# A linear-attention block with its feed-forward on one core: biases folded into the weights, one Relu pass per engine, and the first half reordered

## The chip, the core and the metric

One core of a Trainium2 chip. Its engines run side by side, each with its own queue of instructions in program order: TensorE (PE; matmuls into the banks of PSUM, the accumulator memory, 2 KB per partition each), VectorE (DVE), ScalarE (ACT), GpSimd (POOL) and SyncE (SP), which here issues all DMAs. They meet at semaphores: an instruction adds to one when it ends, and `wait_ge` holds a queue until a count is reached. The metric is the device time of one execution in microseconds; lower is better.

## The reference

```python
xn = _layernorm(x, axis=-1)                                  # x: 8 batches, 1024 tokens, 256 channels, fp32
qkv = (xn @ qkv_w + qkv_b).reshape(b, n, 3, H, D)            # 16 heads of 16
q, k = _l2norm(q), _l2norm(k)
kv = jnp.einsum('bhnd,bhne->bhde', k, v)                     # no softmax
out = jnp.einsum('bhnd,bhde->bhne', q, kv) ... @ proj_w + proj_b
h = jax.nn.relu(xn @ W1 + b1)                                # 1024 wide
return x + out + (h @ W2 + b2)
```

## The kernel before

Work goes in halves `s` of a batch (16 halves, 512 tokens, four tiles of 128); the even half of batch `b` has `u` = 0, the odd one `u` = 1. Each engine has a function `body(b)` that holds one batch in hand-written order; batch 0 and the last are written out, those between run in a loop. In batch 0 the flag `opening` marks its first half.

Every product is made in three: a value is split into `_hi` (rounded to the fast 32-bit format, by a copy) and `_lo` (the rest, by a subtraction), and `product` (L798 on) sums hi·hi, hi·lo and lo·hi. So nearly every tile takes a copy on ScalarE and a subtraction on VectorE or GpSimd before TensorE can use it.

For a half: VectorE takes the variance of x (`variance`) and writes xn (`normalise`, L602, a subtraction and a multiplication per tile); ScalarE makes xn_hi, GpSimd xn_lo (L295). VectorE transposes 32x32 blocks (L609) and SP moves them into place with 16 DMAs (L254); ScalarE and VectorE split xT. The feed-forward goes in eight chunks `j` of 128: `ffn_up` writes W1's chunk times xT into one of two `w_bank`s, ScalarE applies Relu with the bias twice, into h_hi (L444) and back into the bank (L445), VectorE subtracts to h_lo (`h_low`), and `ffn_down` adds h times W2 into `o_bank`. `ffn_up(j)` waits for `h_low(j - 2)`, and `ffn_down(j)` for `h_low(j)`. `query_key(s + 1, ., t)` makes q and k of the next half, tile by tile, into `v_bank`, between the chunks; VectorE adds the bias (L641), ScalarE squares, VectorE sums (L645), `bound` (L651), a root, and `divide` (L663) for k and then for q. q's blocks take the same way by DMA (`transpose_q`, then qT_hi on ScalarE, qT_lo on GpSimd, L332); k is split (k_lo, GpSimd, L307) and summed over the tokens (GpSimd, L315 and L321).

v is never made. `gather` (after chunk 2) sums G = xnᵀk in `g_bank`. In the odd half `key_value` (after chunk 4) makes Wvᵀ G, with two products with `ones` for the sum of k over tokens; ScalarE scales that sum with v's bias (L462), `mask_kv` on VectorE (L675 on) adds it, masks heads and splits; `project` (after chunk 6) multiplies by proj_w, m is split, and `attend` closes the batch with q times m for both halves; VectorE adds the results to y_sb (L694, L705), to which GpSimd added the output's biases (L300), and SP stores them.

At the start (L927 on) TensorE multiplies the identity 17 times, transposes half 0, multiplies it 7 times again, and then makes q and k of half 0 before the first chunk of the feed-forward. SP loads x, wqk, its bias spread over 128 partitions, W1, x of half 1, b1 (element by element) and W2.

## Time and profile before

| | us |
|---|---|
| median of three runs | 637.21 (634.02 to 637.76) |
| the profiled execution | 637.44, its span 635.7 |
| TensorE busy | 583.1 (92%) |
| VectorE busy | 484.0 (76%) |
| ScalarE busy | 285.3 (45%) |
| GpSimd busy | 230.2 (36%) |
| DMA, mean | 71 GB/s |

"Busy" is the time in which an engine has an instruction in work; matmuls overlap, so their durations add up to more than that. Busy shares are of the whole span; the stages are what the groups of rows below are for.

### The profile page before, as it was taken

The numbers are of one execution on the slowest core, as the hardware profiler recorded it, in microseconds if no ns is written. First come the engines' busy times: TensorE is split into PE (matmuls) and PEld (weight loads), VectorE is DVE, ScalarE is ACT, GpSimd is POOL, SyncE is SP. The second block draws the span as 40 slices with busy tenths as digits, with TensorE's granted clock in tenths as the row PEclk, the third lists the DMA queues.
The fourth block names the chain that finished last, engine by engine and source line by source line (L and its number), as shares of the span: only waits on it lengthen the run. The fifth ranks groups of instructions, "written<-read, shape, count | busy, mean of one in ns | idle before, by whom it ended". The sixth has DMA issues, their size and how long they took to land.

```text
span 635.7 us, 10583 instructions
## 1 busy us (share of the span) xinstructions
PE 583.1 (92%) x3648; PEld 522.8 (82%) x3648; DVE 484.0 (76%) x869; ACT 285.3 (45%) x500; POOL 230.2 (36%) x153
## 2 busy tenths in 40 slices
PE   7269999999999998999899999899998999899996
PEld 7259788988888887898788988898877988789896
DVE  5976886968869697887878788696887969785633
ACT  4434526354443645445363543635354463553540
POOL 3633552334313453024533155134440345311360
PEclk9779999999999999999999999999999999999998
DMA  8315122250322503224131422125031241212111
GB/s 248 82 41 143 18 40 61 74 143 17 78 57 54 144 14 76 74 37 128 29 70 66 124 42 66 33 77 144 15 76 51 58 108 19 43 70 38 63 34 66
DMA packets 80355, 44.85 MB, mean 71 GB/s; under 512 B 71376, under 2 KB 73168, under 8 KB 80336
## 3 DMA queue, kind: packets, MB, share of 16 engines
q1 hardware_dynamic: 80336, 44.60, 27.7%
q8 instruction: 11, 0.18, 0.1%
q14 instruction: 8, 0.07, 0.0%
HBM read 20.45 MB, written 8.39 MB: 45 GB/s over the span
## 4 chain that ended last, share of the span: by engine, by line
issue 55%; POOL 18%; DVE 10%; PE 8%; SPq 3%; ACT 2%; DMA 2%; POOLq 0%; DVEq 0%; ACTq 0%
POOL k_sum L321 6%; POOL xn_lo L295 5%; SPq L254 3%; POOL qT_lo L332 3%; POOL y_sb L300 2%; POOL k_sum L315 2%; DMA qk<-qkv_w 1%; DVE qk L641 1%; DVE qk_v L651 1%; DVE xn L602 1%; PE v_bank L800 1%; PE o_bank L800 1%; PE o_bank L802 1%; PE o_bank L801 1%; PE v_bank L801 1%
## 5 line engine op out<-in xcount | busy, mean ns | idle before, releaser
L800 PE MATMUL o_bank<-w_hi,h_hi 128*128 128x256 f32 x512 | 146.3, 286 | 2.7 <-DVE y_sb L705 1.7
L801 PE MATMUL o_bank<-w_lo,h_hi 128*128 128x256 f32 x512 | 145.1, 283 | 0.0
L802 PE MATMUL o_bank<-w_hi,h_lo 128*128 128x256 f32 x512 | 145.0, 283 | 0.0
L553 DVE TENSOR_TENSOR h_lo<-w_bank,h_hi 128x512 fp32r<-128x512 f32 x128 | 87.6, 685 | 61.0 <-ACT w_bank L445 59.4
L800 PE MATMUL w_bank<-xT_hi,w_hi 128*128 128x512 f32 x256 | 102.4, 400 | 26.6 <-DVE h_lo L553 26.3
L444 ACT ACTIVATE h_hi<-w_bank,bias_h 128x512 fp32r<-128x512 f32 x128 | 86.9, 679 | 65.6 <-PE w_bank L802 65.5
L800 PEld LDWEIGHTS o_bank<-w_hi,h_hi 128*128 128x128 f32 x512 | 100.3, 196 | 13.2 <-DVE y_sb L705 3.9
L307 POOL TENSOR_TENSOR k_lo<-qk,k_hi 128x1024 fp32r<-128x1024 f32 x16 | 38.8, 2427 | 185.6 <-ACT k_hi L400 185.6
L430 ACT ACTIVATE qk_sq<-qk 128x512 f32<-128x512 f32 x64 | 40.5, 632 | 145.2 <-DVE qk L641 145.1
L801 PEld LDWEIGHTS o_bank<-w_lo,h_hi 128*128 128x128 f32 x512 | 100.3, 196 | 4.5
L802 PE MATMUL w_bank<-xT_hi,w_lo 128*128 128x512 f32 x256 | 101.5, 397 | 0.0
L801 PE MATMUL w_bank<-xT_lo,w_hi 128*128 128x512 f32 x256 | 100.8, 394 | 0.0
L802 PEld LDWEIGHTS o_bank<-w_hi,h_lo 128*128 128x128 f32 x512 | 100.5, 196 | 0.0
L445 ACT ACTIVATE w_bank<-w_bank,bias_h 128x512 f32<-128x512 f32 x128 | 83.8, 654 | 0.0
L800 PEld LDWEIGHTS w_bank<-xT_hi,w_hi 128*128 128x128 f32 x256 | 48.3, 189 | 38.5 <-issue 17.0
L300 POOL TENSOR_TENSOR y_sb<-y_sb,bias_out 128x1024 f32<-128x1024 f32 x16 | 38.4, 2400 | 104.4 <-DMA y_sb<-x 104.4
L645 DVE TENSOR_REDUCE qk_v<-qk_sq 128x32 f32<-128x512 f32 x64 | 43.8, 684 | 31.2 <-ACT qk_sq L430 31.1
L663 DVE TENSOR_TENSOR qk<-qk,qk_rn 128x1024 f32<-128x1024 f32 x32 | 65.8, 2057 | 0.5
L641 DVE TENSOR_TENSOR qk<-v_bank,bias_qk 128x512 f32<-128x512 f32 x64 | 43.9, 686 | 23.7 <-PE v_bank L802 12.0
L802 PEld LDWEIGHTS w_bank<-xT_hi,w_lo 128*128 128x128 f32 x256 | 48.4, 189 | 10.4
L295 POOL TENSOR_TENSOR xn_lo<-xn,xn_hi 128x1024 fp32r<-128x1024 f32 x16 | 38.4, 2400 | 45.8 <-ACT xn_hi L400 45.8
L800 PE MATMUL v_bank<-wqk_hi,xT_hi 128*128 128x512 f32 x128 | 51.2, 400 | 3.8 <-DVE xT_lo L553 3.5
(121 smaller groups left out, 1155.1 us busy)
## 6 DMA issues: line engine op xcount, KB each, us to landing
qT_lo<-blocks SPq DMA_DIRECT2D x256, 32.0 KB, 1.9
y_sb<-x SPq DMA_DIRECT2D x16, 512.0 KB, 4.3
x_sb<-x SPq DMA_DIRECT2D x15, 512.0 KB, 5.6
xT_raw<-blocks SPq DMA_DIRECT2D x224, 32.0 KB, 1.9
out<-y_sb SPq DMA_DIRECT2D x14, 512.0 KB, 2.7
y_sb<-w SPq DMA_DIRECT2D x1, 1024.0 KB, 10.0
w_raw<-w SPq DMA_DIRECT2D x1, 1024.0 KB, 13.1
out<-y_sb SPq DMA_DIRECT2D x4, 256.0 KB, 2.0
```

The source lines that it names most:

```text
L295: nc.gpsimd.tensor_tensor(xn_lo[:, u], xn[:], xn_hi[:, u].bitcast(F32), ALU.subtract).then_inc(xn_split_done, 1)
L300: nc.gpsimd.tensor_tensor(y_sb[:, u], y_sb[:, u], bias_out[:].unsqueeze(1).to_broadcast([P, TILES, C]), ALU.add).then_inc(y_set, 1)
L430: nc.scalar.activation(qk_sq[:, t % 2, :], qk[:, t, :], ACT.Square).then_inc(qk_sq_done, 1)
L444: nc.scalar.activation(h_hi[:, j % RING, :], w_bank[j % 2][:], ACT.Relu, bias=bias_h[:, j:j + 1])
L445: nc.scalar.activation(w_bank[j % 2][:], w_bank[j % 2][:], ACT.Relu, bias=bias_h[:, j:j + 1]).then_inc(h_done, 1)
L553: return nc.vector.tensor_tensor(to, whole, high.bitcast(F32), ALU.subtract)
L641: nc.vector.tensor_tensor(qk[:, t, :], v_bank[t % 2][:], bias_qk[:], ALU.add).then_inc(qk_biased, 1)
L645: nc.vector.tensor_reduce(qk_v[:, t, :], qk_sq[:, t % 2, :].rearrange("p (h d) -> p h d", d=D), AXIS.X, ALU.add).then_inc(qk_ss_done, 1)
L663: nc.vector.tensor_tensor(part, part, by, ALU.mult).then_inc(done, 1)
L800: nc.tensor.matmul(to, left[0], right[0], start=first, stop=False, skip_group_check=shared)
L801: nc.tensor.matmul(to, left[0], right[1], start=False, stop=False, skip_group_check=shared)
L802: return nc.tensor.matmul(to, left[1], right[0], start=False, stop=last, skip_group_check=shared)
```

## The change

1. Layer norm's rows have the sum zero. The changed kernel writes xn + 0.25 (`SHIFT`), subtracts from each column of W1, wq, wk and wv its mean, and adds bias / (256 x 0.25). The product is then the same with the bias in it. TensorE makes these corrections once, in fp32 (`column_raise`), VectorE adds them to the raw weights before they are split. The bias of q and k, of b1 and of v, the sum of k, its split, its two products and its scaling go away.
2. ScalarE applies Relu once (h_hi); VectorE takes max(., 0) - h_hi in one instruction (h_lo). ScalarE squares q and k out of the bank and copies them (`qk_out`).
3. `normalise` goes to ScalarE (scale and bias per partition; VectorE makes the offset in `spread`), but for half 0; k_lo and qT_lo go from GpSimd to VectorE.
4. The first half is written by hand on each engine (`opening`): the feed-forward starts before q and k, W1 and W2 are loaded in parts, wqk after them; SP moves x's blocks of half 2 ahead of q's of half 0. In the loop VectorE's `mask_kv` stands before `h_low(7)`, and GpSimd's y_sb addition behind xn_lo.

The diff, cut to its core:

```diff
+SHIFT = 0.25
...
+        bias_h = qk_sq[0:1].rearrange("p t n -> p (t n)")
+        xn_first = xT_raw[:].rearrange("p k n -> p (k n)").rearrange("p (t c) -> p t c", t=TILES)
...
-            sp.dma_start(w1_raw, w1.rearrange("(k p) n -> p k n", p=P)).then_inc(w1_loaded, 16)
-            sp.dma_start(x_sb[:, 1, :, :], x_halves[1]).then_inc(x_loaded[1], 16)
...
+            w1_by_chunk = w1.rearrange("(k p) n -> p k n", p=P)
+            for part in range(PARTS):
+                cols = part_columns(part)
+                sp.dma_start(w1_raw[cols], w1_by_chunk[cols]).then_inc(w1_loaded[part], 16)
+            w2_by_chunk = w2.rearrange("(j p) n -> p j n", p=P)
+            sp.dma_start(w2_raw[:, 0:2], w2_by_chunk[:, 0:2]).then_inc(w2_loaded[0], 16)
...
+            def opening():
+                load_x(4, 0)
+                sp.wait_ge(xn_split_done, 2)
+                sp.wait_ge(xT_ready, 2 * KC)
+                move_x(2)
+                load_y(0, 0)
+                load_y(0, 1)
+                move_q(0, 0)
...
-            def sum_k(s, u):
-
-                k = qk[:, :, C:2 * C]
-                wait(pool, k_done, s + 1)
-                if u == 0:
-                    nc.gpsimd.tensor_tensor(k_sum[:], k[:, 0], k[:, 1], ALU.add).then_inc(k_sum_step, 2)
-                    rest = range(2, TILES)
-                else:
-                    rest = range(TILES)
-                for t in rest:
-                    wait(pool, k_sum_step, TILES * s + t)
-                    nc.gpsimd.tensor_tensor(k_sum[:], k_sum[:], k[:, t], ALU.add).then_inc(k_sum_step, 1)
...
+                split_xn(0, 0)
+                split_xn(1, 1)
+                pool.wait_ge(bias_o_loaded, 32)
+                nc.gpsimd.tensor_tensor(bias_out[:], bias_out[:], bias_ffn, ALU.add).then_inc(bias_out_ready, 1)
+                pool.wait_ge(wvp_loaded, 32)
+                nc.gpsimd.tensor_copy(proj_hi[:], proj_raw).then_inc(wvp_hi_ready, 1)
+                pool.wait_ge(wvp_hi_ready, 1)
+                nc.gpsimd.tensor_tensor(proj_lo[:], proj_raw, proj_hi[:].bitcast(F32),
+                                        ALU.subtract).then_inc(wvp_ready, 1)
+                split_xn(2, 0)
+                pool.wait_ge(bias_out_ready, 1)
+                add_bias(0, 0)
...
+            def half(b, s, u, last):
+                if not last:
+                    split_xn(s + 2, u)
+                add_bias(b, u)
...
+                for t in range(TILES):
+                    done = nc.scalar.activation(to[:, t, :], x_sb[:, u, t, :], ACT.Identity,
+                                                bias=ln_offset[:, t:t + 1], scale=ln_rstd[:, t:t + 1])
+                done.then_inc(xn_done, 1)
...
+            def qk_out(s, t):
+
+                wait(act, qk_ready, TILES * s + t + 1)
                 wait(act, qk_ss_done, TILES * s + t - 1)
-                nc.scalar.activation(qk_sq[:, t % 2, :], qk[:, t, :], ACT.Square).then_inc(qk_sq_done, 1)
+                nc.scalar.activation(qk_sq[:, t % 2, :], v_bank[t % 2][:], ACT.Square).then_inc(qk_sq_done, 1)
+                if t == 0:
+                    wait(act, q_transposed, s)
+                    wait(act, k_lo_done, s)
+                copy(qk[:, t, :], v_bank[t % 2][:]).then_inc(qk_copied, 1)
...
-            def h_chunk(s, j):
+            def h_high(s, j):
 
                 wait(act, h_ready, JC * s + j + 1)
-                nc.scalar.activation(h_hi[:, j % RING, :], w_bank[j % 2][:], ACT.Relu, bias=bias_h[:, j:j + 1])
-                nc.scalar.activation(w_bank[j % 2][:], w_bank[j % 2][:], ACT.Relu,
-                                     bias=bias_h[:, j:j + 1]).then_inc(h_done, 1)
+                nc.scalar.activation(h_hi[:, j % RING, :], w_bank[j % 2][:], ACT.Relu).then_inc(h_done, 1)
...
+                nc.vector.scalar_tensor_tensor(ln_offset[:], ln_mean[:], -1.0, ln_rstd[:], ALU.mult,
+                                               ALU.mult).then_inc(ln_product_done, 1)
+                wait(dve, ln_product_done, s + 1)
+                nc.vector.tensor_scalar(ln_offset[:], ln_offset[:], SHIFT, None, ALU.add).then_inc(ln_offset_done, 1)
...
+                nc.vector.tensor_tensor(w1_raw[cols], w1_raw[cols],
+                                        w1_raise[part].unsqueeze(1).to_broadcast([P, KC, 2 * P]),
+                                        ALU.add).then_inc(w1_raised, 1)
...
-                less(h_lo[:, j % RING, :], w_bank[j % 2][:], h_hi[:, j % RING, :]).then_inc(h_lo_done, 1)
+                nc.vector.scalar_tensor_tensor(h_lo[:, r, :], w_bank[j % 2][:], 0.0, h_hi[:, r, :].bitcast(F32),
+                                               ALU.max, ALU.subtract).then_inc(h_lo_done, 1)
...
-                wait(dve, bv_ks_done, b + 1)
-                nc.vector.tensor_tensor(kv[:], kv_raw[:, :, 0, :], bv_ks[:], ALU.add).then_inc(kv_biased, 1)
-                wait(dve, kv_biased, b + 1)
+                wait(dve, kv_ready, b + 1)
+                nc.vector.tensor_copy(kv[:], kv_raw[:, :, 0, :]).then_inc(kv_half_done, 1)
+                wait(dve, kv_half_done, b + 1)
...
+                if ahead:
+                    xT_low(s + 1, 1 - u)
+                k_low(s)
+                h_low(s, 2)
+                divide(0, q_done)
+                transpose_q(s)
+                h_low(s, 3)
+                if not last:
+                    variance(s + 2, b + 1, u)
+                h_low(s, 4)
+                if ahead:
+                    sum_squares(s + 1, 0)
+                if not last:
+                    spread(s + 2)
+                if u == 1:
+                    g_low(b)
+                if not last:
+                    transpose_x(s + 2)
+                h_low(s, 5)
+                if ahead:
+                    sum_squares(s + 1, 1)
+                h_low(s, 6)
+                qT_low(s, u)
+                if ahead:
+                    sum_squares(s + 1, 2)
+                if u == 1:
+                    mask_kv(b)
+                h_low(s, 7)
...
+            def column_raise(to, weights, bias):
+
+                for k in range(KC):
+                    nc.tensor.matmul(to, neg_mean[:], weights[:, k, :], start=k == 0, stop=False)
+                return nc.tensor.matmul(to, bias_weight[0:1, :], bias, start=False, stop=True)
...
-                nc.tensor.matmul(ks_all, ones[:], ks_hi[:], start=True, stop=False)
-                nc.tensor.matmul(ks_all, ones[:], ks_lo[:], start=False, stop=True)
...
             keep_warm(17)
+            raise_w1(0)
+            raise_w1(1)
             transpose_x(0, 0)
-            keep_warm(7)
-            pe.wait_ge(wqk_ready, 1)
-            for t in range(TILES):
-                query_key(0, 0, t)
+            raise_w1(2)
+            raise_w1(3)
...
+                    if j == 0:
+                        pe.wait_ge(w1_raised, PARTS)
+                        pe.wait_ge(wqk_loaded, 16)
+                        pe.wait_ge(bias_qkv_loaded, 16)
+                        column_raise(v_bank[0][:], wqk_raw, bias_qkv[:, 0:2 * C]).then_inc(wqk_raise_done, 1)
+                    if j == 1:
+                        transpose_x(1, 1)
+                    if j == 2 or j == 3:
+                        query_key(0, 0, 2 * j - 4)
+                        query_key(0, 0, 2 * j - 3)
...
+                    if j == 5:
+                        query_key(1, 1, 0)
+                        query_key(1, 1, 1)
+                    if j == 6:
+                        gather(0, 0, 0)
+                        query_key(1, 1, 2)
+                    if j == 7:
+                        query_key(1, 1, 3)
+                        pe.wait_ge(wvp_loaded, 32)
+                        column_raise(kv_bank[:, 0:C], wv_raw, bias_qkv[:, 2 * C:3 * C]).then_inc(wv_raise_done, 1)
```

TensorE, the start of the program, up to the first product of the feed-forward. Before (`w_hi` and `w_lo` are parts of W1, `wqk` the weights of q and k; 24 rows of `v_bank` lie between the fourth row and `w_bank`):

```order
L925 MATMUL kv_bank<-ident 128x128 x17
L817 MATMUL o_bank<-ident,xn 128x128 x8
L925 MATMUL kv_bank<-ident 128x128 x7
L800 MATMUL v_bank<-wqk_hi,xT_hi 128x512
L801 MATMUL v_bank<-wqk_lo,xT_hi 128x512
L802 MATMUL v_bank<-wqk_hi,xT_lo 128x512
```

and now (`y_sb` holds the raw W1 here, `qk_sq` its bias):

```order
L1015 MATMUL w_bank<-ident 128x128 x17
L892 MATMUL g_bank<-y_sb,neg_mean 128x256 x2
L893 MATMUL g_bank<-qk_sq,bias_weight 128x256
L892 MATMUL kv_bank<-y_sb,neg_mean 128x256 x2
L893 MATMUL kv_bank<-qk_sq,bias_weight 128x256
L907 MATMUL o_bank<-ident,xn 128x128 x8
L892 MATMUL v_bank<-y_sb,neg_mean 128x256 x2
L893 MATMUL v_bank<-qk_sq,bias_weight 128x256
L892 MATMUL v_bank<-y_sb,neg_mean 128x256 x2
L893 MATMUL v_bank<-qk_sq,bias_weight 128x256
L877 MATMUL w_bank<-xT_hi,w_hi 128x512
```

The 24 products of q and k are gone from the place between the transposes and the first chunk, and 12 fp32 products stand there.

VectorE, the end of an odd half, from the split of chunk 6 to that of chunk 7 and of kv. Before:

```order
L553 TENSOR_TENSOR h_lo<-w_bank,h_hi 128x512
L641 TENSOR_TENSOR qk<-v_bank,bias_qk 128x512
L645 TENSOR_REDUCE qk_v<-qk_sq 128x32
L553 TENSOR_TENSOR h_lo<-w_bank,h_hi 128x512
L675 TENSOR_TENSOR kv<-kv_bank,bv_ks 128x256
L677 TENSOR_TENSOR kv<-kv_bank,kv 128x256
L679 TENSOR_TENSOR kv<-kv,head_mask 128x256
L681 CAST kv_hi<-kv 128x256
L553 TENSOR_TENSOR kv_lo<-kv,kv_hi 128x256
```

and now:

```order
L719 SCALAR_TENSOR_TENSOR h_lo<-w_bank,h_hi 128x512
L587 TENSOR_TENSOR qT_lo<-qT_lo,qT_hi 128x1024
L686 TENSOR_REDUCE qk_v<-qk_sq 128x32
L728 COPY kv<-kv_bank 128x256
L730 TENSOR_TENSOR kv<-kv_bank,kv 128x256
L732 TENSOR_TENSOR kv<-kv,head_mask 128x256
L734 CAST kv_hi<-kv 128x256
L587 TENSOR_TENSOR kv_lo<-kv,kv_hi 128x256
L719 SCALAR_TENSOR_TENSOR h_lo<-w_bank,h_hi 128x512
```

The five steps of kv now come before the last h_lo and behind qT_lo, which GpSimd made before.

VectorE, the start of a half in the loop: xT of the next half, then what belongs to this one. Before:

```order
L553 TENSOR_TENSOR xT_lo<-xT_raw,xT_hi 128x512
L194 ISA
L553 TENSOR_TENSOR h_lo<-w_bank,h_hi 128x512
L663 TENSOR_TENSOR qk<-qk,qk_rn 128x4x256
L194 REGISTER_ALU
L609 STREAM_TRANSPOSE blocks<-qk 128x2x2x4x32 x2
```

and now:

```order
L587 TENSOR_TENSOR xT_lo<-xT_raw,xT_hi 128x512 x2
L587 TENSOR_TENSOR k_lo<-qk,k_hi 128x1024
L719 SCALAR_TENSOR_TENSOR h_lo<-w_bank,h_hi 128x512
L705 TENSOR_TENSOR qk<-qk,qk_rn 128x4x256
L659 STREAM_TRANSPOSE blocks<-qk 128x2x2x4x32 x2
```

k_lo stands between xT_lo and the h_lo of chunk 2, and so ahead of q's division and transpose.

## Rows read from the trace of the kernel before

**Rows 1.** Stages: start:end, length, then busy us (instructions) per engine, PE clock, DMA.
```profile
0.00:109.30 109.30, 85.19 (x500) 75.44 (x500) 81.83 (x156) 49.50 (x88) 47.45 (x43) 0.92 0.35 92
...
184.40:259.50 75.10, 71.42 (x449) 63.96 (x449) 60.26 (x109) 34.80 (x62) 26.88 (x16) 1.00 0.28 70
...
559.80:625.80 66.00, 63.17 (x414) 57.74 (x414) 37.34 (x56) 27.59 (x47) 21.56 (x14) 0.99 0.19 48
```

**Rows 2.** Waits of PE, 115 to 600 us: total, times, longest.
```profile
PE g_bank L800 <- DVE kv_lo L553: 8.9, 6, 1.5
PE w_bank L800 <- DVE h_lo L553: 8.0, 6, 1.3
PE v_bank L800 <- DVE xT_lo L553: 2.9, 6, 0.5
PE o_bank L800 <- DVE y_sb L705: 1.7, 7, 0.3
```

**Rows 3.** Timeline, PE, opening: start, us, then the instruction [idle before <-releaser].
```profile
17.69 0.40 PE L800 MATMUL w_bank<-xT_hi,w_hi 128*128 128x512 f32 x1
...
20.22 0.40 PE L802 MATMUL w_bank<-xT_hi,w_lo 128*128 128x512 f32 x1
37.20 0.76 PE L800 MATMUL w_bank<-xT_hi,w_hi 128*128 128x512 f32 x1 [16.58 <-DVE h_lo L553]
```

**Rows 4.** Timeline, several engines, an odd half, 162 to 181 us.
```profile
162.23 2.40 POOL L300 TENSOR_TENSOR y_sb<-y_sb,bias_out 128x1024 f32<-128x1024 f32 x1
162.29 2.36 DVE L583 TENSOR_TENSOR ln_m<-ln_parts 128x4 f32<-128x4 f32 x1
...
166.06 0.50 PE L800 MATMUL w_bank<-xT_hi,w_hi 128*128 128x512 f32 x1 [1.34 <-DVE h_lo L553]
...
178.72 0.28 PE L802 MATMUL o_bank<-w_hi,h_lo 128*128 128x256 f32 x1
180.47 0.39 PE L800 MATMUL g_bank<-proj_hi,kv_hi 128*128 128x256 f32 x1 [1.47 <-DVE kv_lo L553]
```

**Rows 5.** Stages, as rows 1: the long stop, and the end of the program.
```profile
24.00:37.00 13.00, 0.00 (x0) 0.00 (x0) 12.59 (x27) 3.85 (x7) 6.18 (x5) 0.50 0.00 1
...
624.00:626.00 2.00, 2.00 (x13) 2.00 (x12) 0.69 (x1) 0.39 (x1) 0.00 (x0) 0.52 0.00 0
```

**Rows 6.** Timeline, POOL and DVE, in the long stop.
```profile
18.48 4.98 POOL L363 TENSOR_TENSOR w_lo<-w_raw,w_hi 128x512 fp32r<-128x512 f32 x4
20.33 6.18 DVE L651 TENSOR_SCALAR qk_v<-qk_v 128x128 f32<-128x128 f32 x1
...
25.71 0.72 POOL L367 TENSOR_TENSOR bias_out<-bias_out,k_sum 128x256 f32<-128x256 f32 x1
```

**Rows 7.** Groups by line and form: count | busy us, mean ns | idle before.
```profile
L553 DVE TENSOR_TENSOR h_lo<-w_bank,h_hi 128x512 fp32r<-128x512 f32 x128 | 87.6, 685 | 61.0 <-ACT w_bank L445 59.4
...
L445 ACT ACTIVATE w_bank<-w_bank,bias_h 128x512 f32<-128x512 f32 x128 | 83.8, 654 | 0.0
L663 DVE TENSOR_TENSOR qk<-qk,qk_rn 128x1024 f32<-128x1024 f32 x32 | 65.8, 2057 | 0.5
...
L641 DVE TENSOR_TENSOR qk<-v_bank,bias_qk 128x512 f32<-128x512 f32 x64 | 43.9, 686 | 23.7 <-PE v_bank L802 12.0 <-POOL k_sum L321 11.5
...
L602 DVE TENSOR_SCALAR xn<-x_sb,ln_mean,ln_rstd 128x256 f32<-128x256 f32 x64 | 24.6, 448 | 1.1
...
L553 DVE TENSOR_TENSOR wqk_lo<-qk,wqk_hi 128x1024 fp32r<-128x1024 f32 x1 | 1.2, 1226 | 0.7 <-ACT wqk_hi L400 0.7
```

**Rows 8.** Timeline, DVE, into an odd half.
```profile
224.87 0.29 DVE L562 SCALAR_TENSOR_TENSOR qk_e<-qk_e,qk_y 128x128 f32<-128x128 f32 x1
...
226.66 1.29 DVE L553 TENSOR_TENSOR xT_lo<-xT_raw,xT_hi 128x512 fp32r<-128x512 f32 x2
```

**Rows 9.** Timeline, PE, second warm-up (fp32).
```profile
9.80 1.73 PE L925 MATMUL kv_bank<-ident 128*128 128x128 f32 x14
```

**Rows 10.** Timeline, SP, last batch: q's blocks.
```profile
605.55 10.27 SPq L254 DMA_DIRECT2D qT_lo<-blocks  x16
```

683 lines of the change are left out of this document (345 added, 338 removed).

## The prediction

> **What bounds the kernel now.** I read the stages first. Cut at the attention products of each batch, the program is an opening of 109.3 us, six batches of 75.1 us that repeat each other, and a last one of 66.0 us with its end behind it [rows 1]. In a middle batch TensorE is busy for 71.4 of 75.1 us, VectorE 60.3, ScalarE 34.8, GpSimd 26.9: TensorE sets the pace, and only its waits can be won. The view of TensorE's waits from 115 to 600 us (6.5 batches) sums to 21.5 us, 3.3 a batch, and all of them end at VectorE: at kv_lo, h_lo, xT_lo and the additions into y_sb [rows 2]. A wait costs more than its idle time, since the pipeline starts afresh. From the start at 17.69 to that at 20.22 lie 11 products of 512 columns, 0.23 us each, and half of that for 256 [rows 3]; the wait for kv_lo shows 1.47 us of idle, and 1.75 us lie between two starts that should be 0.12 apart, so with its slow restart it costs 1.7; the wait for h_lo(4), 1.34 idle, costs 1.6 [rows 4].
>
> The opening is another matter. TensorE issues the last product of the first two chunks at 20.22 us and the next at 37.20: 16.58 us of idle, the longest of the run, and the clock has by then stood at 0.50, the 1.2 GHz level, since 24 (the product at 37.20 takes 0.76 instead of 0.40) [rows 3, 5]. Behind it stands VectorE: `bound` (L651) takes 6.18 us from 20.33, until GpSimd's unbroken run of splits, begun before 18.5, ends with bias_out at 26.43; then come variance, norms, divide and normalise, and only then h_lo [rows 6].
>
> **Why VectorE is late in the loop.** The same pair. GpSimd's y_sb addition runs 162.23 to 164.63, and VectorE's ln_m, 4 elements wide, starts at 162.29 and ends at 164.65; h_lo(4) is behind it, and TensorE waits until 166.06 [rows 4]. `divide` (L663) has a mean of 2.06 us, while the wqk_lo split of as many columns, with no GpSimd beside it, takes 1.23. What reads an operand from PSUM doesn't suffer: h_lo, 0.685 us, mean of 128 [rows 7].
>
> **The change in the loop, per batch.**
> 1. GpSimd loses k_lo, k_sum, ks_lo and qT_lo and keeps four instructions of 2.4 us, 9.6 of 26.9 us [rows 1, 4]. The y_sb addition of the odd half now stands behind xn_lo of a later half and no longer meets the variance; h_lo(4) isn't held: -1.6 us.
> 2. The bias and the scaled k_sum leave the path to kv, and mask_kv stands ahead of h_lo(7), behind qT_lo and one sum of squares. I walk the odd half with the times of this trace, chunk 4 starting at 229.35: ScalarE ends normalise, g_hi and xn_hi at 240.1, h_hi(5) 240.7, h_hi(6) 242.4, waits for q's blocks until 243.4, ends qT_hi at 244.5; GpSimd's y_sb addition holds qT_lo until 245.0, it ends 246.2, kv_lo 248.8. TensorE wants it at 251.2: -1.7 us, with 2.4 in hand. h_lo(7) ends at 249.4, wanted at 252.
> 3. One Relu less (0.654 us, L445) between product and h_lo [rows 7]: the small waits for the y additions and for m_lo go or shrink, -0.5 us. The chain h_lo, add_ffn, norms, divide, xT_lo starts 0.5 us earlier, so that the wait for xT_lo (2.9 us in 6.5 batches, 0.7 a batch with its restart) falls to 0.2: -0.5 us [rows 2].
> 4. Two `ones` products fewer, 0.12 each: -0.2 us.
> 5. Against it: k_lo, 1.23 us, now stands on VectorE between xT_lo and h_lo(2). xT_lo ended at 227.9 [rows 8] and ends at 227.4 now, k_lo at 228.65, h_lo(2) at 229.3; TensorE is ready at 228.9: +0.4 us. In the even half 2.2 us are in hand. q's transpose comes no later, as `divide` isn't held any more.
> 6. Hidden: ScalarE takes over normalise (on VectorE four of 0.448 a half) and the copy of qk, whose additions (0.686) leave VectorE [rows 7]. No row shows either on ScalarE: I take 0.4 and 0.55, by its Relu of 512 columns, 0.65; the floor would be 0.2 and 0.3, the ceiling twice 0.65. It falls behind chunk 5, which has 2 us in hand. VectorE's batch: 60.3 -5.5 -3.6 -3.3 (`divide` four times 0.8) +4.9 (four splits) +0.6 (the offset) = 53 of 71 us.
>
> Sum: -1.6 -1.7 -0.5 -0.5 -0.2 +0.4 = **-4.1 us a batch**, 71.0 instead of 75.1; for six, -24.6. h_lo as a scalar_tensor_tensor from PSUM has no row; its 128x128 form takes 0.29 us, which gives no sign of a lower rate [rows 8], so I take 0.685 as now; the ceiling is twice that (case A).
>
> **The opening.** TensorE gains fp32 products that raise the weights. The warm-up's 14 rows (7 products of 128 columns) take 1.73 us, so 0.25 a product [rows 9]; 256 columns 0.45, 512 columns 0.9. Three products a raise: W1's four 5.3 us, wqk 2.6, wv 1.3, together 9.2; the 7 warm-up products (1.7) go. By steps: the first warm-up ends at 8.1; raises and transposes go on to 14.2 (W1's first quarter comes behind x alone and is there); VectorE adds raise 0 (10.4), raise 1 (11.6), splits w1 (12.3), xT (13.5), so chunk 0 starts 14.2, chunk 1 15.6; h_lo(0) 17.1, so chunk 2 starts 17.2, where it started at 37.2. The raise of wqk is 20.0 to 22.6; q and k slide in behind chunk 2. Waits that I find from there: 0.8 us for transpose_x(1), as spread and normalise are late while GpSimd splits w1 and w2 (15.8 to about 24); 2.4 us at q, k of tile 3, as the variance of half 2 is held by xn_lo, xn_lo, bias_out and proj_lo on GpSimd (32 to 38), and ScalarE's ln_sqrt(2) holds what is behind it; 1.3 at gather, k_lo standing behind both divides, the transpose and h_lo(7); 2.6 at the start of half 1, where ScalarE waits for q's blocks, which SP sends only after x's (16 of them take 10.27 us [rows 10]). With the products counted at 0.23 and 0.12 the attention of batch 0 starts at 98.3 instead of 109.3: **-11.0 us**. Half of these waits would make -15; twice them, with the clock down for some of it, -4.
>
> **The end.** In the last batch q's blocks decide: SP sends them from 605.55 to 615.8, then follow qT_hi, kv and project [rows 10]. k_lo puts the transpose 1.8 us later behind the divide of k, which comes 0.6 earlier; qT_lo stands ahead of kv (1.2), while h_hi(7), h_lo(7) and the scaled k_sum no longer do (-2.1): **+0.3 us**.
>
> **Sum**: 637.4 (this execution: span 635.7 and 1.7 around it; the median 637.21 is the same) -11.0 -24.6 +0.3 = **602 us**.
>
> **Rivals.**
> - A, half of the loop's gain: the waits move to h_lo(2), xT_lo and the y additions, where VectorE's order is as tight as before, or h_lo takes longer; -2.0 a batch: 637.4 -11 -12 +0.3 = 615. For it: step 5, and the norms and divide between the additions into v_bank and o_bank, which stay. Against: 7 us more room on VectorE. 0.15.
> - B, the opening gives 4 only: 609. TensorE's stops of 1 to 2.5 us follow each other there, and after the stop for kv_lo in the last batch the clock is 0.52 for 624 to 626 [rows 5]. 0.17. The Trainium skill (TensorE: Matmul & The Clock Gate, § HAM oscillation — how this bites in real kernels) states that idle gaps which come again and again can throttle the engine anew each time, so that each burst starts at the low level; the row of 624 to 626 agrees, and by that rule the opening would lose case B's 7 us.
> - C, slower: k_lo and qT_lo on VectorE meet GpSimd's kept instructions in every half and are held for all of their 2.4 us [rows 4], 9.6 us a batch. It decides once TensorE pays for more than 5 of these; if it pays for all, 637.4 -11 + 7 x (9.6 - 4.1) = 665. Against: k_lo falls where GpSimd has nothing to do until xn_hi, 12 us later, and of the two qT_lo one meets it. 0.03. The Trainium skill (SBUF — State Buffer, § Who interferes with whom) says that a Vector instruction with two SBUF inputs and a GpSimd one that reads SBUF lock each other out for a whole instruction. ln_m and `divide` agree [rows 4, 7]; k_lo and qT_lo become just such instructions, so the rule speaks for C where they meet.
> - D, the opening has half of my waits: 598. 0.09.
> - E, no effect of note, since the waits come back at the same size elsewhere and the raises eat the opening: 631 to 640. 0.04.
> - My forecast, 598 to 607: 0.52.
>
> **Numbers.** The range takes in the forecast, B, D and A's edge: 595 to 615. A measurement of this kernel can tell about 1% (6 us) from no change: faster 0.92, within 1% 0.05, slower 0.03.
>
> **What would show it.** Middle batches 71 us apart; on TensorE no wait for kv_lo, none for h_lo(4), a new one of 0.3 us for h_lo(2); ln_m under 0.2 us in every half, `divide` at 1.23; the first FFN product at 14 us, chunk 2 near 17, no idle over 3 us; attention 0 at 98. It is wrong if h_lo takes over 0.8 us, if normalise on ScalarE holds h_hi(5) so that TensorE waits at chunk 7, or if q's blocks hold ScalarE and with it h_hi(7).

## The result and the profile after

| | before | after |
|---|---|---|
| median of the runs, us | 636.29 (634.02 to 637.76, 4 runs) | 603.46 (603.03 to 604.65, 4 runs) |
| profiled execution: span | 635.7 | 601.6 |
| TensorE busy, share of the span | 92% | 97% |
| VectorE, ScalarE, GpSimd busy | 76%, 45%, 36% | 69%, 43%, 15% |

The ratio of the medians is 0.949, with a 95% interval of 0.9456 to 0.9524: faster, as forecast, and 1.5 us from the 602 us of the prediction. The sum came out closer than its terms did.

Stages of the changed kernel, cut as in [rows 1]: start:end, length, then busy us (instructions) of TensorE, its weight loads, VectorE, ScalarE and GpSimd, then the granted clock of TensorE, the DMA share and GB/s. The lines are the opening, a middle batch, the last batch and the end.

```profile
0.00:101.70 101.70, 93.34 (x521) 78.78 (x522) 75.79 (x153) 49.95 (x92) 28.97 (x30) 0.98 0.33 96
172.20:242.60 70.40, 70.12 (x447) 63.44 (x447) 49.99 (x102) 32.65 (x60) 9.60 (x4) 1.00 0.27 75
524.50:592.40 67.90, 63.34 (x412) 58.15 (x411) 36.13 (x55) 18.53 (x32) 4.77 (x2) 0.97 0.17 47
592.40:601.60 9.20, 5.95 (x50) 5.75 (x49) 2.77 (x4) 0.00 (x0) 0.00 (x0) 1.00 0.30 114
```

The first attention product of a batch starts at 101.67, 172.15, 242.61, 313.08 and so on to 524.48, and the last at 592.44 us. Against the starts before (109.36, 184.38, 259.40 ... 560.02, 625.78) that splits the 34.1 us by which the span fell:

| stage | before | after | change | predicted |
|---|---|---|---|---|
| opening | 109.36 | 101.67 | -7.7 | -11.0 |
| six batches | 450.66 (75.1 each) | 422.81 (70.47 each) | -27.9 | -24.6 |
| last batch | 65.76 | 67.96 | +2.2 | +0.3 together |
| end | 9.92 | 9.16 | -0.8 | |

TensorE's waits from 115 to 570 us (six and a half batches), which answer to [rows 2] (total, times, longest):

```profile
PE w_bank L877 <- DVE h_lo L719: 1.6, 1, 1.6
PE o_bank L877 <- DVE y_sb L758: 1.4, 6, 0.3
```

Of the 21.5 us of waits before, 3.0 are left, and the first line is one wait, in the last batch. In the loop the waits for kv_lo, h_lo(4) and xT_lo are gone.

The timeline of VectorE, GpSimd and TensorE near the end of an odd half, which answers to the end of [rows 4]:

```profile
230.59 2.42 POOL L334 TENSOR_TENSOR y_sb<-y_sb,bias_out 128x1024 f32<-128x1024 f32 x1
...
232.14 1.95 DVE L587 TENSOR_TENSOR qT_lo<-qT_lo,qT_hi 128x1024 fp32r<-128x1024 f32 x1 [1.25 <-ACT qT_hi L410]
...
236.30 0.42 DVE L587 TENSOR_TENSOR kv_lo<-kv,kv_hi 128x256 fp32r<-128x256 f32 x1
...
239.07 0.28 PE L877 MATMUL g_bank<-proj_hi,kv_hi 128*128 128x256 f32 x1
```

kv_lo ends at 236.72 and TensorE comes to it at 239.07 without having waited, so 2.35 us are in hand; the walk had said 2.4. qT_lo takes 1.95 us, though its usual time is 1.22: it starts while GpSimd's y_sb addition runs and ends about 1.1 us behind it.

Groups by line and form (count | busy us, mean ns | idle before), which answer to [rows 7]:

```profile
L719 DVE SCALAR_TENSOR_TENSOR h_lo<-w_bank,h_hi 128x512 fp32r<-128x512 f32 x128 | 87.3, 682 | 48.5 <-ACT h_hi L468 46.7
...
L705 DVE TENSOR_TENSOR qk<-qk,qk_rn 128x1024 f32<-128x1024 f32 x32 | 39.0, 1221 | 0.5
L587 DVE TENSOR_TENSOR qT_lo<-qT_lo,qT_hi 128x1024 fp32r<-128x1024 f32 x16 | 24.8, 1551 | 17.9 <-ACT qT_hi L410 17.9
...
L587 DVE TENSOR_TENSOR k_lo<-qk,k_hi 128x1024 fp32r<-128x1024 f32 x16 | 19.5, 1221 | 1.1 <-ACT k_hi L410 1.1
```

The one-instruction h_lo costs what the subtraction did (682 ns now, 685 before), and `divide` has fallen from 2.06 to 1.22 us now that nothing on GpSimd runs beside it.

TensorE's timeline (start, us, the instruction, [idle before <- releaser]) in the opening, which answers to [rows 3], and in the last batch:

```profile
7.47 1.03 PE L892 MATMUL g_bank<-y_sb,neg_mean 128*128 128x256 f32 x4
...
14.94 0.50 PE L877 MATMUL w_bank<-xT_hi,w_hi 128*128 128x512 f32 x1
...
18.11 0.47 PE L877 MATMUL w_bank<-xT_hi,w_hi 128*128 128x512 f32 x1
...
39.31 0.50 PE L877 MATMUL v_bank<-wqk_hi,xT_hi 128*128 128x512 f32 x1 [1.15 <-ACT qk L410]
...
72.96 0.48 PE L877 MATMUL v_bank<-wqk_hi,xT_hi 128*128 128x512 f32 x1 [3.60 <-issue]
...
569.24 0.50 PE L877 MATMUL w_bank<-xT_hi,w_hi 128*128 128x512 f32 x1 [1.59 <-DVE h_lo L719]
...
588.69 0.44 PE L877 MATMUL g_bank<-proj_hi,kv_hi 128*128 128x256 f32 x1 [2.65 <-DVE kv_lo L587]
```

Chunk 0 starts at 14.94 (14.2 was said), chunk 2 at 18.11 (17.2), and the idle stretch of 16.58 us is gone. What is left are stops of 1.15 us, of 1.09 (for k_lo, at 53.34) and of 3.60 where half 1 begins, and two in the last batch.

### The profile page after: what moved, and what is told of

It is laid out like the page before. It is cut to its first block, busy times and chain, and to the rows that moved or that the text cites. A ratio compares the mean times of both kernels' runs of the same rounds, so it can differ in the third digit from the quotient of the medians.

```text
span 601.6 us, 10350 instructions
## 1 busy us (share of the span) xinstructions
PE 583.9 (97%) x3654; PEld 523.7 (87%) x3654; DVE 414.3 (69%) x817; ACT 260.1 (43%) x471; POOL 91.3 (15%) x56
## 4 chain that ended last, share of the span: by engine, by line
PE 82%; DVE 10%; issue 3%; SPq 2%; ACT 1%; DMA 0%; DVEq 0%; POOL 0%; POOLq 0%
PE o_bank L877 9%; PE o_bank L878 9%; PE o_bank L879 9%; PE w_bank L877 9%; PE w_bank L878 8%; PE w_bank L879 8%; PE v_bank L877 6%; PE v_bank L878 6%; PE v_bank L879 6%; PE g_bank L877 3%; PE g_bank L878 3%; PE g_bank L879 3%; SPq L272 2%; DVE qk_y L592 1%; DVE y_sb L758 1%
## 5 line engine op out<-in xcount | busy, mean ns | idle before, releaser
L719 DVE SCALAR_TENSOR_TENSOR h_lo<-w_bank,h_hi 128x512 fp32r<-128x512 f32 x128 | 87.3, 682 | 48.5 <-ACT h_hi L468 46.7
L468 ACT ACTIVATE h_hi<-w_bank 128x512 fp32r<-128x512 f32 x128 | 75.1, 593 | 62.4 <-PE w_bank L879 62.4
L329 POOL TENSOR_TENSOR xn_lo<-xn,xn_hi 128x1024 fp32r<-128x1024 f32 x15 | 36.1, 2409 | 388.3 <-ACT xn_hi L410 388.3
L450 ACT ACTIVATE qk_sq<-v_bank 128x512 f32<-128x512 f32 x64 | 38.0, 594 | 77.2 <-PE v_bank L879 77.2
L878 PEld LDWEIGHTS w_bank<-xT_lo,w_hi 128*128 128x128 f32 x256 | 48.5, 189 | 7.6
L879 PE MATMUL v_bank<-wqk_hi,xT_lo 128*128 128x512 f32 x128 | 50.9, 398 | 0.0
L878 PE MATMUL v_bank<-wqk_lo,xT_hi 128*128 128x512 f32 x128 | 50.9, 398 | 0.0
L410 ACT ACTIVATE k_hi<-qk 128x1024 fp32r<-128x1024 f32 x16 | 17.0, 1060 | 70.6 <-DVE qk L705 70.6
```

The costliest lines, as they stand in the source:

```text
L329: nc.gpsimd.tensor_tensor(xn_lo[:, u], xn_of(s), xn_hi[:, u].bitcast(F32), ALU.subtract).then_inc(xn_split_done, 1)
L410: return nc.scalar.activation(to, what, ACT.Copy)
L450: nc.scalar.activation(qk_sq[:, t % 2, :], v_bank[t % 2][:], ACT.Square).then_inc(qk_sq_done, 1)
L468: nc.scalar.activation(h_hi[:, j % RING, :], w_bank[j % 2][:], ACT.Relu).then_inc(h_done, 1)
L719: nc.vector.scalar_tensor_tensor(h_lo[:, r, :], w_bank[j % 2][:], 0.0, h_hi[:, r, :].bitcast(F32), ALU.max, ALU.subtract).then_inc(h_lo_do ...
L878: nc.tensor.matmul(to, left[0], right[1], start=False, stop=False, skip_group_check=shared)
```

## The experiments

Times are medians of four or five executions; the changed kernel is at 603.5 us, and the kernel before, run beside each experiment, had medians between 634.5 and 636.2. The changed kernel was not run again beside them, so a difference of 1 or 2 us to it is read from the stages of the profiled executions. "Batch" is the mean distance of two attention products over the six batches in the middle of the program.

### Which part of the change took the waits away

First the two changes of order that the loop contains, put one at a time and then together into the kernel before, without any folding.

GpSimd's addition behind xn_lo, in the kernel before:

```diff
-                    add_bias(b, u)
-                    if first and u == 0:
+                        add_bias(b, u)
...
                     if not last:
                         split_xn(s + 2, u)
+                    if not (first and u == 0):
+                        add_bias(b, u)
                     qT_low(s, u)
```

> The kernel before with one thing changed: in every half but the first GpSimd adds the output bias to y_sb behind xn_lo instead of ahead of it. Theory (that addition, 2.4 us, holds VectorE's ln_m, and with it h_lo(4)): ln_m under 0.2 us, the wait of 1.34 us for h_lo(4) goes, minus 1.6 us a batch, middle batches 73.5, about 626 us. Rival (VectorE is late there because k_sum on GpSimd holds the bias addition ahead of the variance, 1.26 us of idle): about half of the wait stays, middle batches 74.3, 631 us. Other rival (the held instruction only moves on to qT_lo and kv): 636 us.

Measured: 618.97 us (618.12 to 620.92) where 626 was expected, batches of 72.80 us. TensorE's waits from 115 to 560 us:

```profile
PE g_bank L801 <- DVE kv_lo L554: 6.8, 6, 1.2
PE v_bank L801 <- DVE xT_lo L554: 2.9, 6, 0.5
PE o_bank L801 <- DVE y_sb L706: 1.4, 6, 0.3
```

No wait for h_lo(4) is left, and ln_m has a mean of 154 ns instead of 1122. So the held ln_m was the whole cause of that wait: the hold by k_sum was still there, 1.27 us of VectorE's idle, and TensorE did not wait for it. The gain is 2.3 us a batch, not 1.6: the wait for kv_lo shrank too, from 1.47 to 1.13 us, and one of 0.2 us for the bank of the chunk behind `key_value` went, since VectorE and GpSimd are both earlier from there to the end of the half. With the opening's 2.7 us, this one moved line is worth 16 us.

kv ahead of h_low(7), in the kernel before:

```diff
-                    h_low(s, 7)
                     if u == 1:
                         mask_kv(b)
+                    h_low(s, 7)
```

> The kernel before with one thing changed: the five steps of kv stand ahead of h_low(7). Theory: they start when the scaled sum of k is there, 252.05, and kv_lo ends at 254.1 instead of 255.4; TensorE wanted it at 254.0, so 0.1 of the 1.47 us stays, and h_lo(7) ends at 254.8, ahead of the 256 at which it is wanted: minus 1.5 us a batch, middle batches 73.6, about 626 us. Rival (the ScalarE and GpSimd chain decides, not the order on VectorE): kv_lo as late as before, 636 us.

Measured: 625.52 us (625.28 to 627.49), batches of 74.00 us, a gain of 1.1 a batch and not 1.5. The same view:

```profile
PE w_bank L800 <- DVE h_lo L553: 8.0, 6, 1.3
PE v_bank L800 <- DVE m_lo L553: 4.3, 6, 0.7
```

The wait for kv_lo went altogether, but part of it came back one step on: the products of m come earlier, while m_lo, on VectorE behind h_lo(7), the sums of squares and the first h_lo of the next half, doesn't. I had followed the chain to kv_lo and not to its next user.

Both together:

> The kernel before with both of these changes of order and nothing else: the y_sb addition behind xn_lo, and kv ahead of h_low(7). Theory (two separate waits, each removed by its own move): minus 3.1 us a batch, middle batches 72.0, about 615 us, two thirds of the loop's gain of 4.6 us a batch without any folding of biases. Rival (the folding is needed, the waits come back in another place): 622 us or more.

Measured: 609.94 us (608.74 to 610.18), batches of 71.74 us: 3.4 of the loop's 4.6 us a batch, and 25 of the 33 us of the whole change, from two moves in the order and no folding. Part of kv_lo's wait came back at m_lo, as the rival said, but a small part. Waits:

```profile
PE v_bank L801 <- DVE m_lo L554: 2.9, 6, 0.5
PE v_bank L801 <- DVE xT_lo L554: 2.9, 6, 0.5
```

Now the reverse: each of the two orders taken back in the changed kernel.

```diff
+                h_low(s, 7)
                 if u == 1:
                     mask_kv(b)
-                h_low(s, 7)
```

> The changed kernel with one thing undone: VectorE's five steps of kv stand behind h_low(7) again. Theory (the kv path is short enough by what left it, and the place in the order is a second remedy for the same wait): VectorE ends qT_lo at 234.09 and a sum of squares at 234.7, h_lo(7) then ends at 235.4 and kv_lo at 237.4, while TensorE wants it at 239.07. No wait for kv_lo, middle batches stay at 70.5 us, 603.5 us (602 to 605). Rival (the place in the order is what removed the wait of 1.5 us): the wait comes back, 1.7 us a batch, middle batches 72.2, about 615 us.

Measured: 604.75 us (604.05 to 605.14), batches of 70.46 us: nothing in the loop. In its trace kv_lo ends at 236.91 us, with attention 2 starting 0.4 us earlier than in the changed kernel, so 1.8 of the 2.35 us in hand are left. The 1 us is in the last batch and the end (68.55 and 9.98 us instead of 67.96 and 9.16).

```diff
+                add_bias(b, u)
                 if not last:
                     split_xn(s + 2, u)
-                add_bias(b, u)
```

> The changed kernel with one thing undone: in every half but the first GpSimd's y_sb addition stands ahead of xn_lo again. Theory (without k_lo, the sum of k and its split ahead of it on GpSimd the addition is early enough by itself): both additions of a batch then follow one another from 199.7, the second at about 204.6 to 207.0, away from the variance; it may hold the 0.23 us bound at 205.4 until 207, but what is behind it has 3 us in hand; ln_m stays under 0.2 us in the loop, no wait for h_lo(4), middle batches 70.3 to 70.6, 603.5 us (602 to 605). Rival (the place in GpSimd's order is what removed the wait): ln_m 2.4 us and the wait of 1.3 us for h_lo(4) back, 1.6 us a batch or more, 614 us.

Measured: 605.64 us (604.29 to 606.27), just above the 602 to 605 expected, batches of 70.47 us. Nothing in the loop again; the second addition now starts at 207.98 and holds `bound` instead, which has time. The timeline of GpSimd and VectorE there:

```profile
207.98 2.38 POOL L334 TENSOR_TENSOR y_sb<-y_sb,bias_out 128x1024 f32<-128x1024 f32 x1
...
208.36 2.09 DVE L692 TENSOR_SCALAR qk_v<-qk_v 128x128 f32<-128x128 f32 x1
```

The 2 us that it did lose are in the opening (104.67 us, though this execution also began its first raise of W1 1.5 us later), where the addition now meets xT_lo of half 2, on which TensorE waits (5.74 us of idle there instead of 3.60). The same view:

```profile
70.89 3.32 POOL L334 TENSOR_TENSOR y_sb<-y_sb,bias_out 128x1024 f32<-128x1024 f32 x1
...
71.93 3.42 DVE L587 TENSOR_TENSOR xT_lo<-xT_raw,xT_hi 128x512 fp32r<-128x512 f32 x2
```

So each of the two waits has two remedies in the change. The order alone removes it (with 0.5 us for m_lo in the place of kv_lo's), and so does the rest of the change, with that one place undone. What in the rest does it was not separated; what it takes off GpSimd (k_lo, the sum of k) and off the path to kv is the likely part. "The order brought 3.4 us a batch" is measured for both places together, "the order brings nothing in the loop" for each of them alone; a changed kernel with both undone was not run.

### What the Relu and the places of the splits are worth

ScalarE's second Relu put back into the changed kernel, and VectorE's plain subtraction:

```diff
-                nc.scalar.activation(h_hi[:, j % RING, :], w_bank[j % 2][:], ACT.Relu).then_inc(h_done, 1)
+                nc.scalar.activation(h_hi[:, j % RING, :], w_bank[j % 2][:], ACT.Relu)
+                nc.scalar.activation(w_bank[j % 2][:], w_bank[j % 2][:], ACT.Relu).then_inc(h_done, 1)
...
+                less(h_lo[:, r, :], w_bank[j % 2][:], h_hi[:, r, :]).then_inc(h_lo_done, 1)
```

> The changed kernel with ScalarE's second Relu, back into the bank, put back, and VectorE's h_lo a plain subtraction again. Theory (the Relu of 0.65 us bought back the small waits, for y_sb, m_lo and at the start of the odd half, and no more; kv_lo has over 2 us in hand): plus 0.5 to 0.9 us a batch, middle batches 71.2, no wait for kv_lo, about 608 us (606 to 610). h_lo 0.68 us in both forms. Rival 1 (those waits went with the sum of k and the biases): middle batches stay at 70.5, 604 us. Rival 2 (the second Relu held the kv path): a wait for kv_lo of over 1 us a batch, 613 us or more.

Measured: 606.50 us (605.70 to 607.35), between the expectation and its first rival, batches of 70.95 us, plus 0.48. In the loop the whole of it is one wait that stands there again as in [rows 2]. TensorE's waits from 115 to 560 us:

```profile
PE v_bank L877 <- DVE xT_lo L588: 2.9, 6, 0.5
```

So in the loop the Relu paid for the wait for xT_lo and nothing else; the waits for the first y_sb additions and m_lo stayed away without it. The prediction had booked them to it.

k_lo and qT_lo by GpSimd again, in all halves but the first (VectorE's two calls leave `half`):

```diff
             def half(b, s, u, last):
+                wait(pool, k_hi_done, s + 1)
+                nc.gpsimd.tensor_tensor(k_lo[:], qk[:, :, C:2 * C], k_hi[:].bitcast(F32),
+                                        ALU.subtract).then_inc(k_lo_done, 1)
                 if not last:
                     split_xn(s + 2, u)
                 add_bias(b, u)
+                wait(pool, qT_hi_done, KC * (s + 1))
+                half = (slice(None), u)
+                nc.gpsimd.tensor_tensor(qT_lo[half], qT_lo[half].bitcast(F32), qT_hi[half].bitcast(F32),
+                                        ALU.subtract).then_inc(qT_lo_done, 1)
```

> The changed kernel with k_lo and qT_lo of every half but the first made by GpSimd again (2.4 us each there, 1.22 on VectorE). Theory (moving them was about neutral: they were beside the path): h_lo(2) no longer stands behind k_lo, but divide for q is held by k_lo on GpSimd, 1.2 becomes about 2 us, and one xT_lo in the even half too; middle batches 70.3 to 70.9, 603 to 606 us. Rival (the splits on GpSimd were part of what TensorE waited for): plus 1 us a batch or more, 611 us or above, with waits behind divide, xT_lo or qT_lo.

Measured: 600.46 us (600.08 to 601.21), *faster* than the changed kernel by 3 us, and outside of the 603 to 606 expected. By stages: opening +1.7 (103.41; its stop at half 1 has grown to 5.74 us), batches 70.30 (-0.17 each), last batch 64.03 instead of 67.96. GpSimd's k_lo does hold VectorE as expected. The timeline of GpSimd and VectorE in the last batch, with `divide` for q:

```profile
568.10 2.37 POOL L398 TENSOR_TENSOR k_lo<-qk,k_hi 128x1024 fp32r<-128x1024 f32 x1 [8.65 <-ACT k_hi L417]
...
569.14 2.41 DVE L712 TENSOR_TENSOR qk<-qk,qk_rn 128x1024 f32<-128x1024 f32 x1
```

xT_lo rises from a mean of 0.68 to 1.31 us as well. But what is held there is not waited for, while k_lo and qT_lo on VectorE stand ahead of h_lo(2) and kv_lo, which are. In the middle batches that is nearly even; in the last batch it is not.

Normalisation of halves 3 to 15 on VectorE again:

```diff
                 if not last:
                     ln_sqrt(s + 2)
-                    normalise(s + 2, u)
...
                 if not last:
                     spread(s + 2)
+                    wait(dve, ln_offset_done, s + 3)
+                    wait(dve, xn_split_done, s + 2)
+                    for t in range(TILES):
+                        done = nc.vector.tensor_scalar(xn[:, t, :], x_sb[:, u, t, :], ln_rstd[:, t:t + 1],
+                                                       ln_offset[:, t:t + 1], ALU.mult, ALU.add)
+                    done.then_inc(xn_done, 1)
```

> The changed kernel with the normalisation of halves 3 to 15 on VectorE again (four of 0.41 us a half instead of ScalarE's four of 0.52 to 0.59). Theory (either engine has room there, VectorE is at 50 of 70.5 us a batch): middle batches 70.5, 603.5 us (602 to 605). Rival (VectorE's order is tight, work on it shows): 1.4 us later for g_lo, the transposes and h_lo(5) in each half, a wait of TensorE for one of them, plus 0.7 us a batch or more, 608 to 612 us.

Measured: 603.80 us (599.40 to 604.43), batches of 70.46 us. That edit is neutral; its profiled execution, the one of 599.4, is looked at under the clock below.

### The opening's stop

ScalarE's and VectorE's work on q's blocks of half 0 leaves the end of `opening` on both engines and stands in the middle of half 1:

```diff
-                qT_high(0, 0)
...
                 if ahead:
                     qk_out(s + 1, 0)
+                if isinstance(s, int) and s == 1:
+                    qT_high(0, 0)
                 h_high(s, 4)
...
-                qT_low(0, 0)
...
                 h_low(s, 4)
+                if isinstance(s, int) and s == 1:
+                    qT_low(0, 0)
```

> The changed kernel with one thing moved: ScalarE's qT_hi and VectorE's qT_lo of half 0, which wait for q's blocks on the DMA queue, stand in the middle of half 1 instead of ahead of it. Theory (TensorE's stop of 3.6 us at 69.2 is xT_lo behind qT_lo behind qT_hi behind those blocks, and the low clock until 77 follows from it): xT_lo then ends at 69.8, two waits of 0.6 us are left, the clock stays at 1.0, attention 0 at 97.5 instead of 101.7, minus 4.2 us, 599.3 us. Rival (the end of divide and the raise of wv decide, xT_lo is late anyway): under 1.5 us, 602 us or more.

Measured: 599.70 us (598.90 to 601.88), 3.8 less than the changed kernel. The stop is cut in two shorter ones. TensorE's timeline there:

```profile
71.78 0.47 PE L879 MATMUL v_bank<-wqk_hi,xT_hi 128*128 128x512 f32 x1 [0.90 <-issue]
...
74.56 0.50 PE L879 MATMUL w_bank<-xT_hi,w_hi 128*128 128x512 f32 x1 [1.15 <-DVE h_lo L720]
```

Attention 0 starts at 100.33, but this execution also began its first raise of W1 1.5 us later (8.94 against 7.47), so the opening from there is 91.4 instead of 94.2 us. So the cause was the chain that the expectation names; the two waits left are 0.9 and 1.15 us and not 0.6 each. Not all of the 2.8 us is the move's: two kernels with the stop of 3.60 us untouched, the last one above and the next one below, kept the clock in their profiled executions and passed from 71.69 to attention 0 in 27.5 us, where the changed kernel took 28.7 from 72.96. The move itself is then worth some 1.6 us and the clock 1.2.

### The last batch

Only the last half reordered:

```diff
+                if not ahead:
+                    h_high(s, 2)
                 k_high(s)
-                h_high(s, 2)
+                if ahead:
+                    h_high(s, 2)
...
-                k_low(s)
-                h_low(s, 2)
+                if ahead:
+                    k_low(s)
+                    h_low(s, 2)
                 divide(0, q_done)
+                if not ahead:
+                    h_low(s, 2)
                 transpose_q(s)
+                if not ahead:
+                    k_low(s)
```

Where `ahead` is false, `qT_high(s, u)` stands behind `m_high(b)` and `qT_low(s, u)` behind `m_low(b)`, in the same manner.

> The changed kernel with the last half alone reordered: h_hi(2) and h_lo(2) ahead of the split of k, q's division and transposes ahead of k_lo, and qT_hi and qT_lo behind h_lo(7) and m_lo, so that nothing of kv stands behind q's blocks on the DMA queue. Theory (the two stops of the last batch, 1.59 us for h_lo(2) and 2.65 us for kv_lo, and the low clock behind the second, are k_lo and qT_lo, which the change put on VectorE ahead of them): both stops go, the last batch (attention 6 to attention 7) takes 62 to 63 us instead of 67.96, minus 5 to 6 us, 598 us (597 to 599.5). Rival (the gather of G waits for k_lo, or attention for qT_lo, as long): minus 2 us at most, 601.5 or more.

Measured: 598.55 us (595.61 to 598.80). The last batch takes 62.47 us instead of 67.96, and of its stops one of 0.37 us is left. TensorE's timeline:

```profile
565.46 0.50 PE L891 MATMUL w_bank<-xT_hi,w_hi 128*128 128x512 f32 x1 [0.37 <-DVE h_lo L725]
```

So these places cost 5.5 us where the clock falls behind the second stop. In this execution it did not fall; beside the run with VectorE's normalisation, which kept it too with both stops in place (last batch 66.21 us), the reordering is worth 3.7. The kernel before took 65.76 us here and stopped too, 2.04 us for kv_lo.

### All together

Both of the last two, and two moves in `opening`:

```diff
                 qk_out(0, 0)
-                ln_sqrt(2)
                 qk_out(0, 1)
+                ln_sqrt(2)
...
+                k_low(0)
                 transpose_q(0)
                 h_low(0, 7)
-                k_low(0)
```

> The last half of the run before this one in the list, with three moves in the opening of the changed kernel: qT_hi and qT_lo of half 0 in the middle of half 1, ScalarE's root for the variance of half 2 behind q and k of tile 1, and k_lo of half 0 ahead of q's transposes. Theory: the gains add: 4 us of the opening's stop at 69 (2.8 where the clock does not fall in either), 2.3 us of the stops of 1.15 and 1.09 us at 38 and 52, and 5.5 us of the last batch: 592 us (590 to 594). Rival (one of the opening's stops only moves on to half 1): 595 us.

Measured: 593.32 us (593.01 to 594.07); ratio to the kernel before 0.936 (0.9336 to 0.9384). Attention 0 starts at 96.56, the last batch takes 62.46 us, and the clock is 1.00 throughout both.

The same with GpSimd's k_lo and qT_lo from half 2 on:

```diff
             def half(b, s, u, last):
+                second = isinstance(s, int) and s == 1
+                if not second:
+                    wait(pool, k_hi_done, s + 1)
+                    nc.gpsimd.tensor_tensor(k_lo[:], qk[:, :, C:2 * C], k_hi[:].bitcast(F32),
+                                            ALU.subtract).then_inc(k_lo_done, 1)
...
```

> As the last one, but k_lo and qT_lo of all halves from 2 on by GpSimd, and qT_hi of the last half right behind h_hi(7). Theory (in the loop the splits on VectorE cost 0.17 us a batch, by the run that had them on GpSimd; in the last batch VectorE is then free of both): middle batches 70.3, last batch 62 us, 591 us (589 to 593). Rival (GpSimd's k_lo, 2.4 us, holds the division for q, 1.2 becomes 2.4 us, and with it q's blocks of the last half): as the run before or 1 us slower, 592 to 593.

Measured: 592.96 us (591.72 to 593.18); ratio 0.9344 (0.9319 to 0.9369). Batches of 70.30 us, opening 97.50, last batch 62.46. GpSimd's splits give 1 us in the six batches. The opening is the same program in both and yet 0.9 us longer here, with a stop of 0.70 us for k_lo: in this execution a VectorE instruction of four columns was held and in the other it was not (the last section shows such a pair). So between the two runs nothing can be told. By their ratios to the kernel before, both are some 1.5% faster than the changed kernel.

## Why the prediction was right, and where it was not

**The loop, -4.1 us a batch said, -4.6 measured.** Term by term:

1. GpSimd's addition and h_lo(4), -1.6: the size is right (the wait and its restart were 1.6 us, and are gone), ln_m behaves as said in the loop (under 0.2 us). The step named the new place behind xn_lo as what does it; the last undo shows that in the changed kernel, with k_lo and the sum of k gone from GpSimd, that place doesn't matter in the loop. The prediction gave both facts in one sentence and didn't ask which of them was enough.
2. kv_lo, -1.7 with 2.4 us in hand: as said, 2.35 in hand. Again the place ahead of h_lo(7) was not needed for it.
3. The Relu, -0.5 for the small waits and -0.5 for xT_lo: the mechanism for xT_lo is shown (0.48), the booking of the other half isn't; those waits went with the rest.
4. The `ones` products, -0.2: the block around them (two products with `ones`, eight of Wvᵀ G) took 1.31 us from 245.39 to 246.70 and takes 0.88 now, -0.43. The two products are 0.23 of that, as said; the other 0.2 is a wait for the next chunk's bank, which the kernel before with only GpSimd's addition moved had lost as well. The wait for m_lo, 0.4 with what followed it, is part of step 3.
5. k_lo ahead of h_lo(2), +0.4: what shows at the start of an odd half is 0.2 us before the product that needs xT_lo, and 0.3 around h_lo(2), 0.5 together, where 0.75 stood before. The run with GpSimd's splits prices the move as a whole at +0.17 a batch: the term was too large.
6. Hidden: ScalarE's normalisation costs 0.52 us for a tile (2.08 for four; 0.4 was taken), its copy of qk 0.59 (0.55), and the run that moved normalise shows it hidden. VectorE has 50.0 busy us in a batch, where 53 were said.

Of rival A (the waits come back in other places) nothing shows in the changed kernel, but the kernel before with one order changed did just that with m_lo, for 0.7 us. Rival C (GpSimd holds the new splits) is there in small: qT_lo is held for 0.7 us in each odd half, where there is slack, and 1 us in the opening, where there is none. The Trainium skill (SBUF — State Buffer, § Who interferes with whom) gives the lock only to certain pairs of instructions; the traces agree for the pairs shown here: 2.41 against 1.22 us for `divide`, 3.42 for an xT_lo pair of 1.28, and h_lo, with its operand in PSUM, at 0.68 in every kernel.

**The opening, -11.0 said, -7.7 measured.** The steps were right, and the walk of waits names each stop that the trace has; two of its signs failed, attention 0 at 98 (101.67) and no idle over 3 us (3.60). Sizes missed on two terms. The raises take more: the four of W1 1.6 us each instead of 1.3, wqk 2.9 instead of 2.6, wv 1.6 instead of 1.3, together 1.8 us; I had scaled the price of a 128 column product and left the start of each group out. And the stop at half 1, for which 2.6 us were said, is 3.6 idle with a restart, and then TensorE runs at the 1.2 GHz level for some 3.5 us, 5.3 us in all. Against it, the stops at 27 and at 38 cost less than said (0.4 and 1.3, instead of 0.8 and 2.4), and the first warm-up ended 0.6 us earlier; some 0.9 us of the 3.3 are spread over small ones. The prediction named ScalarE's wait for q's blocks at half 1; in the trace VectorE's qT_lo comes behind it and takes 2.2 us beside GpSimd's wv_lo, and xT_lo, which TensorE waits for, stands behind both:

```profile
69.45 2.20 DVE L587 TENSOR_TENSOR qT_lo<-qT_lo,qT_hi 128x1024 fp32r<-128x1024 f32 x1 [0.91 <-ACT qT_hi L410]
71.58 1.28 DVE L587 TENSOR_TENSOR xT_lo<-xT_raw,xT_hi 128x512 fp32r<-128x512 f32 x2
```

Part of the miss is this execution's. The kernel with only the last half reordered has the same opening, and its profiled execution reached attention 0 at 99.16: no stop at 38, and no fall of the clock. Beside that one, the forecast is off by 0.8 us.

**The end, +0.3 said, +1.4 measured** (+2.2 in the last batch, -0.8 behind it, since the low clock after the stop for kv_lo now lies ahead of the attention product). The path was the right one: followed back from the end of the program, the chain of work runs through kv_lo, kv, qT_lo, qT_hi, q's blocks on the DMA queue, the transposes, `divide`, h_lo(2), k_lo and k_hi. What failed is its sum. Counted from attention 6, `divide` for k starts 0.7 us earlier (0.6 was said), q's transposes start 1.7 us later (1.2 was said, 1.8 less 0.6), the sixteen DMAs take 11.16 us instead of 10.27 (nothing was said; executions of this batch show 10.26 to 11.16), and from there to kv the path is 1.1 us shorter (0.9 was said): kv_lo ends 1.4 us later. The transposes come later than said because VectorE also stands still before k_lo, which must wait for k_hi there:

```profile
567.36 1.23 DVE L587 TENSOR_TENSOR k_lo<-qk,k_hi 128x1024 fp32r<-128x1024 f32 x1 [1.13 <-ACT k_hi L410]
...
571.68 11.16 SPq L272 DMA_DIRECT2D qT_lo<-blocks  x16
```

TensorE's stop of 1.59 us for h_lo(2) is new as well, and the prediction had not asked for it in this half: TensorE has no q and k to make between the chunks here, so h_lo(2) is wanted about 1.4 us earlier than in the loop. But nothing of the chain from `divide` for k to kv_lo waits for TensorE, so this stop only takes from the longer one for kv_lo behind it and adds nothing to the time.

The three errors (+3.3, -3.3 and +1.1) happen to leave about 1 us, which is luck. The forecast's sum is no evidence that each term was known.

## What to carry to other kernels

Before a structural change is credited, put its changes of order alone into the old kernel, and take them out of the new one: here two moves were worth 25 of 33 us in the first, and either of them, taken out of the second, nothing in the loop. When a step moves on an in-order queue, redo its arithmetic in every stage that has other cover, the last iteration above all, with what the step must wait for at its new place and not only its own length, and follow the chain one user beyond the wait that goes. And look at what GpSimd runs beside VectorE by the instruction, not by the busy share: a hold costs only where something waits behind it, so a slower place off the path beats a faster one on it.
